# Weights of a third softmax spread over the partitions: four fp32 products, or a diagonal of rows in high and low part

## The reference

```python
s = (c @ w_c + b_c)[:, :, None] + (q @ w_q + b_q)[:, None, :] + cq
a = softmax(s, axis=2)
c2q_att = einsum('bcq,bqd->bcd', a, q)
b_att = softmax(max(s, axis=2), axis=1)            # the third softmax: one row of 112 weights per batch
q2c_att = einsum('bc,bcd->bd', b_att, c)[:, None, :]
x = concat([c, c2q_att, c * c2q_att, c * q2c_att], axis=-1)
z = x @ W_l.T + b_l
```

## Time and profile before

| | us |
|---|---|
| median of 3 runs | 676.71 |
| the profiled execution, its own time | 676.74 |
| its span, first to last instruction | 674.9 |
| TensorE busy | 653.2 (97%) |
| VectorE busy | 486.5 (72%) |
| ScalarE busy | 341.6 (51%) |
| GpSimd busy | 249.4 (37%) |
| mean granted TensorE clock | 0.992 |

### The profile page before, as it was taken

The page is one execution under the profiler, slowest core; times in us unless marked ns, Lnnn a source line. Parts: engine busy times, 40 slices in busy tenths (PEclk is TensorE's granted clock), DMA queues, the critical chain, the costliest instruction groups (busy, mean ns, idle before and its releaser), DMA issues. The chain is left out here.

```text
span 674.9 us, 11730 instructions
## 1 busy us (share of the span) xinstructions
PE 653.2 (97%) x3848; PEld 556.0 (82%) x3848; DVE 486.5 (72%) x1262; ACT 341.6 (51%) x794; POOL 249.4 (37%) x322
## 2 busy tenths in 40 slices
PE   5999999999999999999998989999999999999997
PEld 3868988889788887897886878888888888888886
DVE  5688778878787787887889968765767666577433
ACT  4664766566656665566575444333423335234321
POOL 2146264353561734536533222323222232332331
PEclk8999999999999999999999889999999999999999
DMA  7625044051340431514614260413222133310400
GB/s 209 163 72 153 20 115 123 20 163 53 88 142 7 119 118 39 163 34 118 182 43 121 81 214 1 156 64 126 93 90 91 40 125 93 125 64 2 151 6 32
DMA packets 51790, 64.44 MB, mean 95 GB/s; under 512 B 3928, under 2 KB 49544, under 8 KB 50864
## 3 DMA queue, kind: packets, MB, share of 16 engines
q1 hardware_dynamic: 51760, 64.06, 31.2%
HBM read 56.60 MB, written 7.45 MB: 95 GB/s over the span
## 5 line engine op out<-in xcount | busy, mean ns | idle before, releaser
L1588 POOL TENSOR_TENSOR xt<-xt,cw_wide 128x512 f32<-128x512 f32 x55 | 72.1, 1310 | 178.7 <-ACT xt L1546 178.7
L1612 DVE TENSOR_TENSOR res<-bank,xt 128x512 f32<-128x512 f32 x61 | 41.9, 687 | 57.7 <-POOL xt L1588 53.3
L1550 ACT ACTIVATE a_hi<-res 128x512 fp32r<-128x512 f32 x42 | 26.6, 634 | 99.2 <-DVE res L1612 99.2
L75 PE MATMUL bank<-h_hi,w_lo 128*128 128x512 f32 x168 | 67.6, 402 | 1.6 <-DVE w_lo L1629 0.8
L76 PE MATMUL bank<-h_lo,w_hi 128*128 128x512 f32 x168 | 66.2, 394 | 0.0
L77 PE MATMUL bank<-h_hi,w_hi 128*128 128x512 f32 x168 | 66.0, 393 | 0.0
L75 PE MATMUL bank<-w_hi,op_lo 128*128 128x256 f32 x184 | 53.3, 290 | 0.5 <-DVE op_lo L1128 0.5
L76 PE MATMUL bank<-w_lo,op_hi 128*128 128x256 f32 x184 | 51.4, 280 | 0.0
L77 PE MATMUL bank<-w_hi,op_hi 128*128 128x256 f32 x184 | 51.4, 279 | 0.0
L1617 DVE TENSOR_TENSOR a_lo<-res,a_hi 128x512 fp32r<-128x512 f32 x42 | 33.6, 800 | 22.4 <-ACT a_hi L1550 22.4
L1006 POOL TENSOR_TENSOR wz_lo<-tmp,wz_hi 128x512 fp32r<-128x512 f32 x28 | 35.0, 1282 | 37.6 <-DVE tmp L1171 37.6
(11 more groups left out here) (240 smaller groups left out, 2041.0 us busy)
## 6 DMA issues: line engine op xcount, KB each, us to landing
cw_wide<-in_ctx_t SPq DMA_DIRECT2D x32, 375.0 KB
ctxf<-in_ctx SPq DMA_DIRECT2D x32, 375.0 KB
cw_wide<-cw_scratch SPq DMA_DIRECT2D x7, 1536.0 KB, 7.8
xt<-in_x SPq DMA_DIRECT2D x8, 448.0 KB, 3.9
x_scratch<-x2b SPq DMA_DIRECT2D x8, 448.0 KB, 3.3
x2n<-x_scratch SPq DMA_DIRECT2D x7, 512.0 KB, 4.7
cw_wide<-cw_scratch SPq DMA_DIRECT2D x7, 512.0 KB, 4.2
x2t<-x_scratch SPq DMA_DIRECT2D x7, 512.0 KB, 4.0
```

Source lines behind the costliest of these rows:

```text
L75: pe.matmul(dst, a_lo, b_hi, start=first, stop=False, **kw)
L1550: act.activation(a_hi[n % (AHEAD + 1)][:, :], af[(p + n) % 2][:, :], ACT.Copy).then_inc(a_hi_ok, 1)
L1588: pool.tensor_tensor(sg[b][:, :], sg[b][:, :], cw_wide[p][:, ORDER[n], :], ALU.mult).then_inc(sgw_ok, 1)
L1612: dve.tensor_tensor(af[b][:, :], u_bank[b][:, :], sg[b][:, :], ALU.mult).then_inc(af_ok, 1)
```

## The change

`mrow` becomes a diagonal of rows: on partition p it holds 4 x 112 values, the weights of batch p in block p and zeros elsewhere, made by one VectorE instruction that multiplies mexp (repeated), 1/sum and a loaded 4 x 4 diagonal (repeated). ScalarE rounds it to fp32r (`mrow_hi`), VectorE forms the rest (`mrow_lo`), and TensorE spreads all four rows at once by two fp32r matmuls of 448 columns with a 4 x 128 tile of ones as weights. They stand later in TensorE's program, behind `z_c2q(3)`.

```diff
-            mexp, mrow = sb("mexp", [G, L]), sb("mrow", [G, L])
+            mexp, mrow = sb("mexp", [G, L]), sb("mrow", [G, G, L])
+            mrow_hi, mrow_lo = sb("mrow_hi", [G, G, L], F32R), sb("mrow_lo", [G, G, L], F32R)
+            diag, ones4 = sb("diag", [G, G]), sb("ones4", [G, P], F32R)
...
+                sp.dma_start(diag[:, :], diag_in).then_inc(diag_in_ok, 16)
...
                     z_c2q(1)
-                    pe.wait_ge(mrow_ok, i + 1)
-                    for j in range(G):
-                        last = pe.matmul(m_bank[:, j * L:(j + 1) * L], ident[0:G, j:j + 1].to_broadcast([G, P]), mrow[:, :],
-                                         start=True, stop=True)
-                    last.then_inc(b_mm, 1)
                     z_x3(0)
...
                     z_c2q(3)
+                    if is_first(i):
+                        pe.wait_ge(ones_ok, 1)
+                    pe.wait_ge(mrow_lo_ok, i + 1)
+                    pe.matmul(m_bank[:, 0:TOK], ones4[:, :], mrow_lo[:, :, :].rearrange("p g t -> p (g t)"), start=True, stop=False)
+                    pe.matmul(m_bank[:, 0:TOK], ones4[:, :], mrow_hi[:, :, :].rearrange("p g t -> p (g t)"), start=False, stop=True).then_inc(b_mm, 1)
...
                     x_high(2)
+                    act.wait_ge(mrow_ok, i + 1)
+                    act.activation(mrow_hi[:, :, :], mrow[:, :, :], ACT.Copy).then_inc(mrow_hi_ok, 1)
                     x3_high(1)
...
-                    dve.tensor_scalar(mrow[:, :], mexp[:, :], minv[:, 0:1], None, ALU.mult).then_inc(mrow_ok, 1)
+                    if is_first(i):
+                        dve.wait_ge(diag_in_ok, 16)
+                    dve.scalar_tensor_tensor(mrow[:, :, :], mexp[:, :].unsqueeze(1).to_broadcast([G, G, L]), minv[:, 0:1],
+                                             diag[:, :].unsqueeze(2).to_broadcast([G, G, L]), ALU.mult, ALU.mult).then_inc(mrow_ok, 1)
...
                     x3_low(1)
+                    dve.wait_ge(mrow_hi_ok, i + 1)
+                    dve.tensor_tensor(mrow_lo[:, :, :], mrow[:, :, :], f32(mrow_hi[:, :, :]), ALU.subtract).then_inc(mrow_lo_ok, 1)
                     x_low(3)
...
+                dve.memset(f32(ones4[:, :]), 1.0).then_inc(ones_ok, 1)
```

More of the change, by code:

```diff
@@ L393, in decoder_layer @@
             t_m, mneg_ok, mexp_ok, minv_ok, mrow_ok = sem("m_transposed"), sem("m_max"), sem("m_exp"), sem("m_inv_sum"), sem("b_att_rows")
+            mrow_hi_ok, mrow_lo_ok, diag_in_ok, ones_ok = sem("b_att_rows_hi"), sem("b_att_rows_lo"), sem("diagonal_in"), sem("ones_set")
             b_mm, cb_ok = sem("b_att_widened"), sem("c_times_b_att")
```

## The result

The changed kernel takes 686.37 us (median of four runs, 685.09 to 686.87) against 676.86 us (676.7 to 677.91) for the kernel before, timed beside it: a ratio of 1.0138, 95% interval 1.0121 to 1.0155. Forecast were 681.9 us and a range of 674.5 to 686.0, so the sign came out as forecast and the size did not. The profiled execution took 686.07 us with a span of 684.3 (before: 676.74 and 674.9).

What follows compares the result with a forecast made beforehand. TensorE looked binding at 97% busy, but VectorE's delayed second chain was taken to outweigh its gain. Loop groups +3.1, group 0 +1.1 and the last +1.0 summed to +5.2 on 676.74: 681.9 us, range 674.5 to 686.0.

Steps and rivals of the forecast that it cites:

- What bounds: Loop group: TensorE's side gains 0.15 us, but VectorE's chain grows 0.79 less 0.28 slack, lengthening the passage by 0.51.
- mrow asks 0.02 before its add, so I take -0.14: VectorE, loop group: the new mrow runs at once, 0.61 us instead of 0.75, without waiting for GpSimd's add.
- the other bound: VectorE's mrow waits for the same GpSimd add as before and pays extra elements and form on top: +0.43 us.
- The first rival: mrow waits for the same add as before, 0.57 us more per loop group: 685.3 us, chance 0.18.
- a wait for x3_low(0) near 1.1 us: Sign on TensorE in the loop groups that mrow waits as before; the forecast itself expected 0.5 to 0.6 us.
- mrow_lo, 0.53 + 0.4: VectorE, behind x3_low(1): 0.53 us of work plus an estimated 0.4 waiting for a GpSimd add, bounds 0 and 0.8.
- The second rival: mrow_lo doesn't wait because VectorE keeps the ports between two instructions in a row: +2.2, 678.9 us, chance 0.22.
- The chain's slack of 0.28: VectorE and ScalarE chain over residual, bias, maxima and exps: 0.10 + 0.18 us to spare before TensorE waits.
- 2 x 0.21 = 0.42 us: TensorE behind z_c2q(3): cost of the two added fp32r matmuls of 448 columns, with no wait of their own.
- Group 0 and the last: Group 0: +1.1 us from mrow and mrow_lo less slack. Last group: +1.0, bounds -3.4 and +2.5, partly for low clock.
- 6 x 0.51 + 1.1 + 1.0 = 5.2: Whole kernel: six loop groups, group 0 and the last group together add 5.2 us, giving 681.9.
- It decides from the point where mrow_lo with its wait adds less than 0.27 us: Loop-group threshold on VectorE below which the faster rival holds: only TensorE's side counts, 674.0 us, chance 0.22.

Runs made afterwards that it cites:

- x3 before h: Reordered kernel with mrow and diagonal in PSUM and 128-partition spreading tiles, x3_high(0) and x3_low(0) moved ahead of the next group's h_high_pair(0) and h_low_pair(0): 676.66 us.
- 128 rows: Changed kernel with mrow_hi, mrow_lo and the ones made 128 partitions high, the added rows of mrow_hi and mrow_lo zero: 687.05 us.
- residual last: The "x3 before h" kernel with ScalarE doing h_high_pair(1) ahead of the residual instead of behind it: 671.33 us.
- mrow in PSUM: Changed kernel with mrow written into the spreading's PSUM bank, so mrow_lo has one SBUF input; mrow still reads two: 681.69 us.
- both in PSUM: Changed kernel with mrow written into PSUM and the 4 x 4 diagonal copied into PSUM each group: 679.07 us.
- without low part: Changed kernel without mrow_lo and its matmul, the weights spread from their high part alone: 680.62 us.
- reordered, PSUM: Changed kernel with mrow behind x3_low(1), mrow_lo behind x3_low(3), mrow_hi behind x3_high(2), spreading behind z_x3(2), and mrow and diagonal in PSUM: 679.05 us.
- before, residual last: Kernel before the change, with only ScalarE's h_high_pair(1) moved ahead of the residual: 676.25 us.
- diagonal in PSUM: Changed kernel with the 4 x 4 diagonal copied into PSUM each group, so mrow has one SBUF input: 682.35 us.

## Why the prediction was wrong

*What bounds.* Right. Two chains run through a loop group, TensorE's own and VectorE's over the residual to the probabilities, and the later one counts. The period should grow by the larger of TensorE's shift and the chain's less 0.28, the slack that I read. That gives 1.33 for after (measured 1.37), 0.64 (0.72), 0.75 (0.79), 0.19 (0.23), 0.57 (0.58), 0.81 (0.82), 0.56 (0.61), 0.10 (0.16), 0.05 (0.01) and -0.01 (-0.02) for the kernels of the table down to "x3 before h", and 1.33 (1.29) for 128 rows. The last pair shows the chain as a cause: "residual last" gains only where TensorE's side is ahead.

*"mrow asks 0.02 before its add, so I take -0.14."* This is the step that failed. mrow asked 0.02 before its add in after as well (232.35 against 232.37) and still waited for it: 1.16 us instead of 0.75, +0.41, against the +0.43 worked out for the other bound. It was wrong to hold the two x3_low against it: all eight mrow of before had waited, and the rows of the instruction itself were the nearer ones. Why the two differ stays open. The distances don't tell them apart: x3_low(1) of before asked at 231.61, 0.06 us before an add ended (230.53 + 1.14 = 231.67) and 0.02 before the next began, and didn't wait; mrow stood 0.06 before the end of c_lo and 0.02 before its add, and did. It went so in all six loop groups of before, for both, with distances that differ by no more than 0.02. What differs in these rows is the instruction of GpSimd that was ending, an add there and c_lo here, and no run separates that from the form of mrow. The first rival, 685.3 us, is the case that came, and its marker "a wait for x3_low(0) near 1.1 us" was seen (0.96 of recorded idle time, 1.12 from start to start). Worth 0.55 us in a loop group, more than half of what was missing.

*mrow_lo, 0.53 + 0.4.* Direction and mechanism right, shown by its fall to 0.605 with mrow in PSUM; the wait was 0.55, not 0.4. Beside it x3_low(1) took 0.12 more. The second rival (it doesn't wait) fell.

*The chain's slack of 0.28.* Right: 1.61 - 1.34 = 0.27 in the group of the timelines. After's third low part there is taken by TensorE as soon as it ends, 255.48 + 0.88 = 256.36, and the matmul starts at 256.41 and takes 0.39 instead of 0.28:

```profile
255.48 0.88 DVE L1134 SCALAR_TENSOR_TENSOR op_lo<-bank,sinv,op_hi 128x256 fp32r<-128x256 f32 x2 [0.24 <-ACT op_hi L811]
```

```profile
256.41 0.39 PE L75 MATMUL bank<-w_hi,op_lo 128*128 128x256 f32 x1
```

In the earlier trace rows 0.24 us lay between the two.

*"2 x 0.21 = 0.42 us" for the spreading on TensorE.* Mis-sized: 0.69, and 0.09 on the next matmul, +0.79 in all. The term came from matmuls of 128 rows, while these have four; with 128 rows it holds (0.40). And z_x3(0) starts 0.03 us earlier in its group than before, where the forecast had 0.57: mrow's wait took that. TensorE's side lost 0.75 where I forecast a gain of 0.15. In after this cost nothing, because the chain cost more; by the rule above it sets the period in "mrow in PSUM", "both in PSUM", "without low part" and "reordered, PSUM".

*Group 0 and the last.* Group 0: +1.1 forecast, +0.9 measured. Last: +1.0 forecast, with mrow +0.40 (1.785 against 1.382), as priced, and TensorE's wait 2.51 (forecast 2.5). But mrow_lo ran ahead of x_low(3) into GpSimd's 2.04 us; before, it was only the later x3_low(2) that waited there. The clock did not stay low for longer. In the last group the granted clock falls once in either kernel, after TensorE's waits, and over the five us that hold its fall it is 0.66 in both, 1.7 us of full clock lost. (Over the whole last group it is 0.84 over 11.0 us, before 0.83 over 9.8.) VectorE, TensorE and GpSimd there, and the windows of after:

```profile
374.53 1.78 DVE L1315 SCALAR_TENSOR_TENSOR mrow<-mexp,minv,diag 4x448 f32<-4x448 f32 x1
...
376.54 1.96 DVE L1166 TENSOR_TENSOR op_lo<-tmp,op_hi 128x224 fp32r<-128x224 f32 x1
...
379.33 2.24 DVE L1325 TENSOR_TENSOR mrow_lo<-mrow,mrow_hi 4x448 fp32r<-4x448 f32 x1
```

```profile
378.56 0.37 PE L75 MATMUL bank<-wl_hi,op_lo 128*112 128x256 f32 x1 [2.51 <-DVE op_lo L1166]
```

```profile
373.72 2.12 POOL L1049 TENSOR_TENSOR c_lo<-ct,c_hi 128x896 fp32r<-128x896 f32 x1 [6.61 <-DVE h L195]
...
379.06 2.04 POOL L1036 TENSOR_TENSOR wqkv_lo<-w_f,wqkv_hi 128x768 fp32r<-128x768 f32 x1
```

```profile
373.00:384.00 11.00, 7.48 (x43) 6.50 (x44) 10.78 (x20) 4.50 (x11) 7.38 (x6) 0.84 0.21 63
379.00:384.00 5.00, 4.99 (x26) 4.22 (x25) 4.78 (x10) 2.16 (x4) 2.10 (x2) 0.66 0.00 0
```

The window of before that holds its fall:

```profile
371.00:376.00 5.00, 5.00 (x31) 5.00 (x31) 4.90 (x11) 3.00 (x5) 3.34 (x3) 0.66 0.00 0
```

From the last mark to the end it is +1.8. Behind the last x3_low VectorE is 1.6 us later than before, counted from the mark (382.94 - 369.50 = 13.44 against 373.81 - 361.97 = 11.84), so the waits alone can explain most of it. But this stretch also varies between executions: "before, residual last" has the code of before there and takes 311.5 us for it against 313.0. The +1.8 is therefore no firm number.

*The sum.* Forecast were 6 x 0.51 + 1.1 + 1.0 = 5.2. Measured were 5 x 1.37 + 1.6 + 0.9 + 1.8 = 11.2, less 1.8 of start-up: the span's 9.4. The six loop groups came to 6.9 + 1.6 = 8.5 where 3.1 were forecast. Of these 5.4, 6 x 0.55 = 3.3 is mrow and 6 x 0.27 = 1.6 mrow_lo and its neighbour; the other 0.5 is not taken apart. So the cause is mrow's wait first and mrow_lo's size second; the term for the last group, +1.0, can't be judged to better than the variation of its stretch.

*"It decides from the point where mrow_lo with its wait adds less than 0.27 us."* The other side was never near: with both waits gone the chain is still +0.38.

## What to carry over

Work taken off the busiest engine is a gain only where that engine works without a wait: here 0.7 of the removed 1.15 us covered a wait, and moving the old spreading alone cost 0.82 us per group. Where an instruction of VectorE has waited beside a busy GpSimd, count on its successor at the same place waiting too, and put one operand in PSUM if a bank is free. When an engine gains time and the kernel doesn't, look for the other chain in the waits behind it; here two steps of ScalarE in the wrong order held back all of the gain, and the swap was worth nothing until the first chain had become shorter.

## What the runs showed of the hardware

*Who is served when VectorE and GpSimd both want SBUF.* mrow takes 0.658 us in eight of eight with one of its two tensors in PSUM, 0.947 to 1.785 with both in SBUF; mrow_lo takes 0.605 against 1.148. The Trainium skill, page "SBUF — State Buffer", section "Who interferes with whom", names a VectorE instruction on two SBUF operands beside a GpSimd instruction as the case of contention, and says that the order of issue decides who blocks. The first part agrees with these lines. (The words "for the whole instruction", which the prediction takes up, stand there for the two-port perf modes.) It isn't the only case, though: mrow of before reads a single tensor and one scalar per partition, all in SBUF, and waited too (0.528 to 1.382 us).

The order is clear only where mrow asks well ahead of c_lo's end. Counting back its 0.59 us (its step without a wait, in "diagonal in PSUM") from the start of the next instruction, it was served at 375.65 in the last group, where it asked at 374.53, and at 50.79 - 0.59 = 50.20 in group 0, where it asked at 49.92: each time 0.18 to 0.19 us ahead of c_lo's recorded end (375.84, 50.38). In the loop group it asked 0.06 us ahead of that end and was served only at 233.51 - 0.59 = 232.92, again 0.18 ahead of a recorded end, that of the add behind (233.10). So it lost a whole turn. But x3_low(1) of before asked as close to the end of an add and lost nothing, so closeness alone doesn't decide it. An x3_low that asked in the middle of the adds of the last group waited over several of them (1.96 us, before 2.14). Both stay open.

*Four rows.* Two fp32r matmuls of 448 columns cost 0.79 us with four rows among matmuls of 128 (0.69 and 0.09 on the matmul behind them, rounded), and 0.40 with 128 rows of which 124 are zero.

*A slower first matmul.* In the loop groups looked at, the matmul of 256 columns that follows a wait of TensorE for an operand is recorded with 0.37 to 0.39 us instead of 0.28 and holds the next one up by 0.09 to 0.1. A wait isn't needed for it: behind the four-row matmuls of after it is 0.37 and 0.09 as well.
